# A graph network on one Trainium2 core: the root product and bias of the first relation layer become the initial value of its sums

## What is computed

```python
def rgcn_conv(x, edge_index, edge_type, W, W_root, b):
    src, dst = (edge_index[0], edge_index[1])
    seg = dst * N_REL + edge_type
    x_src = x[src]
    summed = jax.ops.segment_sum(x_src, seg, num_segments=N_NODES * N_REL)
    cnt = jax.ops.segment_sum(jnp.ones((src.shape[0],), x.dtype), seg, num_segments=N_NODES * N_REL)
    agg = summed / jnp.maximum(cnt, 1.0)[:, None]
    agg = agg.reshape(N_NODES, N_REL, x.shape[1])
    return jnp.einsum('nrd,rdh->nh', agg, W) + x @ W_root + b
...
x = jax.nn.relu(rgcn_conv(x, edge_index, edge_type, W1, root1, b1))
x = rgcn_conv(x, edge_index, edge_type, W2, root2, b2)
```

## Time and profile before

| | before |
|---|---|
| median of three runs | 8099.41 us |
| the profiled execution | 8102.81 us |
| its span, first to last instruction | 8100.9 us |
| GpSimd busy | 4914.7 us, 61% |
| TensorE busy (matmul) | 4193.5 us, 52% |
| VectorE busy | 2132.5 us, 26% |
| ScalarE busy | 1985.1 us, 25% |
| mean granted TensorE clock | 0.626 of full speed |

### The profile page before, as it was taken

One profiled execution on the slowest core, in us unless ns is written; L12 is line 12 of the kernel. 1 busy time (PEld: TensorE's weight loads), 2 busy tenths in 40 slices (PEclk: granted clock), 3 DMA queues, 4 the chain that ended last, 5 costly groups with the idle time before them and its releaser, 6 DMA issues.

```text
span 8100.9 us, 98203 instructions
## 1 busy us (share of the span) xinstructions
PE 4193.5 (52%) x18185; PEld 3399.4 (42%) x18186; DVE 2132.5 (26%) x7442; ACT 1985.1 (25%) x5480; POOL 4914.7 (61%) x5319
## 2 busy tenths in 40 slices
PE   5756667773333466666678333335433335333336
PEld 3355666533333345555544333333433334333334
DVE  6643333332222246666633000002000001000002
ACT  1100000010000034444422333331333332333331
POOL 0157777437777647777600777771677774777772
PEclk9956555786556566666657655556555655555556
DMA  4412222252222123333302222220122221222221
GB/s 162 162 39 57 58 57 58 98 211 52 52 52 52 43 61 85 84 84 84 76 0 112 66 52 52 52 52 14 53 52 52 52 52 34 55 52 52 52 52 30
DMA packets 282533, 529.06 MB, mean 65 GB/s; under 512 B 120299, under 2 KB 165695, under 8 KB 269519
## 3 DMA queue, kind: packets, MB, share of 16 engines
q0 software_dynamic: 159744, 330.88, 16.6%
q1 hardware_dynamic: 117918, 193.47, 6.8%
q10 hardware_dynamic: 4656, 2.79, 0.1%
HBM read 377.76 MB, written 149.02 MB: 65 GB/s over the span
## 4 chain that ended last, share of the span: by engine, by line
POOL 47%; issue 27%; PE 16%; DVE 5%; DMA 2%; DVEq 1%; ACT 1%; POOLq 1%; SPq 0%; ACTq 0%
POOL GB L585 45%; PE PS L872 3%; PE PS L1088 3%; PE PS L932 2%; PE PS L981 2%; PE PS L949 2%; PE PS L955 2%; POOL H L585 1%; DVE TOUT L1241 1%; DMA table<-TOUT 1%; DVEq L418 1%; PE PS L884 1%; DVE TOUT L1484 0%; DMA GB<-table_gat,IDX 0%; DVE H L1492 0%
## 5 line engine op out<-in xcount | busy, mean ns | idle before, releaser
L585 POOL DMA_INDIRECT GB<-table,IDX x4160 | 3946.2, 949 | 1426.4 <-issue 1354.8
L884 PE MATMUL PS<-OH,GB 128*128 128x128 f32 x8320 | 1953.2, 428 | 3054.8 <-DMA GB<-table,IDX 3033.5
L884 PEld LDWEIGHTS PS<-OH,GB 128*128 128x128 f32 x8320 | 1802.1, 328 | 3203.2 <-issue 2820.5
L1261 DVE TENSOR_TENSOR ACC<-ACC,PS 128x128 f32 x666 | 190.0, 285 | 4547.1 <-PE PS L884 4543.0
L684 ACT COPY IDX<-idx 128x8 int32 x520 | 102.3, 197 | 4103.4 <-PE PS L884 4103.1
L674 ACT ACTIVATE OH<-iota_f,local 128x128 f32<-128x128 f32 x2496 | 761.9, 387 | 0.0
L579 POOL COPY STG<-X 128x128 f32 x200 | 64.3, 322 | 1061.9 <-DVE X L1294 601.8
L585 POOL DMA_INDIRECT H<-table_gat,IDX x416 | 420.0, 1010 | 126.8 <-issue 124.3
L585 POOL DMA_INDIRECT GB<-table_gat,IDX x416 | 416.4, 1001 | 127.6 <-issue 120.7
L1088 PE MATMUL PS<-TOUT,OH 128*128 128x144 f32 x1664 | 425.9, 448 | 1.1 <-DVE TOUT L1484 1.1
L1088 PEld LDWEIGHTS PS<-TOUT,OH 128*128 128x128 f32 x1664 | 393.6, 329 | 2.7 <-issue 1.2
(11 more groups left out here) (248 smaller groups left out, 4111.0 us busy)
## 6 DMA issues: line engine op xcount, KB each, us to landing
table<-TOUT SPq DMA_DIRECT2D x100, 1024.0 KB, 3.9
GB<-table,IDX POOLq DMA_INDIRECT x4160, 2.5
TOUT<-local_row SPq DMA_DIRECT2D x104, 256.0 KB
table<-TOUT SPq DMA_DIRECT2D x50, 512.0 KB, 2.6
H<-etype_row SPq DMA_DIRECT2D x105, 64.0 KB
GB<-table_gat,IDX POOLq DMA_INDIRECT x416
H<-table_gat,IDX POOLq DMA_INDIRECT x416
table<-TOUT SPq DMA_DIRECT2D x20, 320.0 KB, 2.5
```

The source lines that it names most:

```text
L585: pool.indirect_dma_start(out=out[:, j, :], out_offset=None, in_=r.table.dram[:, :], in_offset=bass.IndirectOffsetOnAxis(ap=idx[:, j:j + 1 ...
L884: return nc.tensor.matmul(PS[:, bank, 0:P], GB[:, b, j * r.width:j * r.width + P], oh(b, j), **at)
```

## The change

The clearing of `sums` goes. After the degree products and before the first round, TensorE multiplies `X` by `root1` chunk by chunk into PSUM banks 1 to 7 in turn, and VectorE, behind the inversion of the counts, writes each chunk plus bias to `sums`. TensorE waits for all 16 of these before the round. Behind the round the node stage is replaced by 16 relus from `sums` to `H`, and the second table waits for those.

```diff
-        n_l0a = Stage("n_l0a", 2, 1, 0)
+        begun_pe, begun_dve, relu_dve = sem("begun_pe"), sem("begun_dve"), sem("relu_dve")
...
-        t_l0b = Table("t_l0b", H, WR[:, 0:2048], table16, [n_l0a.end(), (w2_in, 16)])
+        t_l0b = Table("t_l0b", H, WR[:, 0:2048], table16, [(relu_dve, CHUNKS), (w2_in, 16)])
...
+            for c in range(CHUNKS):
+                if c >= 7:
+                    pe.wait_ge(begun_dve, c - 6)
+                nc.tensor.matmul(PS[:, 1 + c % 7, 0:CHUNK], mat("L0_gnn_root1"), X[:, c * CHUNK:(c + 1) * CHUNK],
+                                 start=True, stop=True).then_inc(begun_pe, 1)
+            pe.wait_ge(begun_dve, CHUNKS)
+
             pe.wait_ge(rt_ready, 2)
...
-            node_products(n_l0a, [(0, mat("L0_gnn_root1"), X)], [], [edges_done(r_l0a)])
             multiply_table(t_l0b)
...
             dve.wait_ge(scratch, 64)
             dve.wait_ge(base_in, 80)
-            dve.memset(sums, 0.0)
             dve.memset(aux[0:R16, :], 0.0)
...
             dve.reciprocal(aux[0:R16, :], aux[0:R16, :]).then_inc(rt_ready, 1)
+
+            for c in range(CHUNKS):
+                dve.wait_ge(begun_pe, c + 1)
+                dve.tensor_scalar(sums[:, c * CHUNK:(c + 1) * CHUNK], PS[:, 1 + c % 7, 0:CHUNK], vec("L0_gnn_b1"), None, ALU.add)\
+                    .then_inc(begun_dve, 1)
+            dve.wait_ge(begun_dve, CHUNKS)
...
-            with dve.Fori(0, PAIRS) as i:
-                st = n_l0a
-                for h in range(2):
-                    dve.wait_ge(st.pe, st.pe_at(i, 1, h))
-                    dve.scalar_tensor_tensor(T0[h], bank(0, h), vec("L0_gnn_b1"), sums[:, chunk(i, h)], ALU.add, ALU.add).then_inc(st.dve, 1)
-                for h in range(2):
-                    dve.wait_ge(st.dve, st.dve_at(i, 1, h))
-                    dve.tensor_scalar(H[:, chunk(i, h)], T0[h], 0.0, None, ALU.max).then_inc(st.dve, 1)
+            dve.wait_ge(r_l0a.agg_free, TWO + TILES)
+            for c in range(CHUNKS):
+                here = slice(c * CHUNK, (c + 1) * CHUNK)
+                dve.tensor_scalar(H[:, here], sums[:, here], 0.0, None, ALU.max).then_inc(relu_dve, 1)
```

More of the change, by code:

```diff
@@ L823, in _ @@
                 pe.sem_inc(t.made, 2)
-            for st in (n_l0a, n_l0b, n_l1, n_l2a, n_l2b, n_l3a, n_l3b):
+            for st in (n_l0b, n_l1, n_l2a, n_l2b, n_l3a, n_l3b):
                 pe.sem_inc(st.pe, 1)
```

## The result

The changed kernel took 8290.57 us (median of 5 runs, 8282.36 to 8298.45) against 8099.41 of the kernel before in the same comparison: a ratio of 1.024, 95% interval 1.0229 to 1.0252. It is slower by 191 us where 17 fewer were forecast, and far outside the range of 8066 to 8097. The profiled execution took 8294.1 us, its span is 8292.2 us.

The account below looks back on a forecast made before the run. GpSimd's gathers were taken to set the edge rounds' pace, with the change acting only in seams between stages. -6.9 + 9.7 - 22.8 + 2.2 = -17.8 us gave 8082 us against 8099.4, range 8066 to 8097.

Parts of the forecast that it names:

- seams: Places between stages where one's end releases the next; the edited ones, with the clock, were to sum to -17.8 us.
- Start: Start of the first table: without clearing `sums`, VectorE is earlier; 6.9 us saved, bounds 5.4 and 8.2.
- Initial value: Ahead of the first edge round: 16 evictions behind the inversion delay the look-ups; 9.7 us added, bounds 5.8 and 15.0.
- Behind the round: Between last addition and first staging copy: 28.02 us of node stage give way to 5.2 us, 22.8 saved.
- Clock: Second table: without the removed stage's warming, TensorE starts at the low clock; 2.2 us lost.
- rival C: VectorE's instruction stream: moved attention loop's returns take longer, up to 8159 us; chance 0.12, of it 0.07 over 0.2% slower.
- the short loops of the other rounds show no such stall: In rival C: only the attention loop's returns, 3.2 us each, showed VectorE standing still with nothing waited for.
- 33 instructions ahead of the round: In rival C: VectorE's program grows by some 33 instructions there, a few behind it, so every later loop moves.
- 24 x 3.2: Rival C's price in the attention loop: returns twice as long add 77 us.
- 8159 us: Rival C's time if each attention loop return needs twice as long, 77 us on top.
- chance of 0.07: Chance given to a time over 0.2% longer, through rival C's longer attention loop return.
- if a stage without any edit gets longer: Sign against the prediction: it is wrong if any unedited stage gets longer or shorter; no size given.

Follow-up runs that it names:

- the one without the stream's effect: Changed kernel plus 1 idle semaphore increment ahead of the first table and 111 ahead of the degree sums; 8087.06 us against 8113.6 before, 0.997.
- before_m2: Kernel before with two VectorE semaphore increments moved behind the first table's loop, which then starts at 319; 8281.26 us, 1.0223.
- before_g20: Kernel before with 20 idle increments ahead of VectorE's wait for the degree sums, attention loop on a border; 8098.31 us, 1.000.
- before_s432: Kernel before with 111 idle increments ahead of the first table and 17 ahead of the degree sums, first loop at 432; 8095.9 us, 0.9996.
- one and four fillers: Changed kernel with one or four semaphore increments nobody waits for ahead of the first table; 8106.97 us (1.0011) and 8076.01 us (0.9968) against the kernel before.
- 16 fillers: Kernel before with 16 idle increments ahead of the degree sums, attention loop 4 instructions ahead of a border; 8130.2 us, 1.0036.
- 433: Kernel before with 112 idle increments ahead of the first table and 16 ahead of the degree sums, first loop at 433; 8212.09 us, 1.0139.
- 440: Kernel before with 119 idle increments ahead of the first table and 9 ahead of the degree sums, first loop at 440; 9835.71 us, 1.015.
- 447: Kernel before with 126 idle increments ahead of the first table and 2 ahead of the degree sums, first loop at 447; 9887.42 us, 1.0189.

## Why the prediction was wrong

**The sum of the seams was right**, -20.0 us against -17.8, though in the initial value two errors met by luck. Part by part, forecast and then the trace of the kernel after:

- Start: -6.9, bounds 5.4 and 8.2; measured -7.8 at block 2 (and -7.0 at the inversion of the kernel whose loop isn't disturbed). Block 1 started at 75.57 and took 3.67 us, the gain from the shorter pause included.
- Initial value: +9.7; measured +9.5. The evictions ended 10.0 us behind the inversion (forecast 10.7). The two errors: each eviction took 0.60 us, from 9.61 / 16 of both rows, and not 0.55, and TensorE, on the 9 chunks left, was hardly behind (it kept VectorE waiting 0.49 us). Batch 0 gave back 0.6 us (look-ups 3.77 to 3.51, sums 3.75 to 3.46) and not 1.0: it was warm only in part.
- Behind the round: -22.8; measured -23.1 (28.02 to 4.89 from the last addition's end). Relus 4.53 us (forecast 4.5), the wait for the own addition 0.03 (0.35), the wake-up 0.33 (0.34).
- Clock: +2.2; measured +1.4 in the kernel after and +2.9 in the one without the stream's effect. The second table starts with weight loads of 0.34 us and reaches 0.19 at 1737.28, 3.2 us after its start. By the Trainium skill (TensorE: Matmul & The Clock Gate, What's actually happening) the slow state is the default, and this trace agrees. But the forecast took from one trace that the removed stage leaves TensorE at the high clock. In three of the seven traces of kernels that keep it (`before_m2`, `before_g20`, `before_s432`) the second table too has first weight loads of 0.34 us, and takes 173.0 us from first to last matmul instead of 171.3 (172.8 in the kernel after, 174.2 in the one without the stream's effect). So a part of this term is there without the change.

**The step that failed is rival C.** It had the right mechanism (the instruction stream), and failed in three of its terms. First its place: it looked at the attention loop alone, since only that one stalled in the trace of before, and let the others go with "the short loops of the other rounds show no such stall". That none stalled showed that each was held from one return to the next, not that it would stay so when moved: the first table's loop stood at 321, and at 319 it stalls. Second its direction: it counted what the change adds (33 instructions ahead of the round), and not the two that it takes away ahead of the first table, which decided 183 us. (The attention loop itself moved by 16.) Third its price: "24 x 3.2" for a longer return was near for the attention loop (a second stall of 3.0 us at 23 returns, 68.5 us), but most of that is hidden, for the round grew by 18.7 us only; and for the first table's loop, which lies on the path, a return cost 8.0 us, 183 us in all: a pause of 8.0 that covers a wait of 2.2, and 2 more through TensorE's lower clock. The 8159 us that it named were thought of as its far end.

The chance of 0.07 for a time longer by over 0.2% was therefore too low by its own reasoning: that the place of loops in the stream weighs was seen, and "nothing in the trace says how the place weighs" should have widened the range, as for any cost that no row bounds.

What the forecast said would prove it wrong, "if a stage without any edit gets longer", is what happened, twice.

**What stays open.** The +4.8 us between the second table and the attention table in the kernel after have no cause that was shown. From last matmul to first matmul that stretch took 1156.8 us there, 1156.2 and 1157.3 with one and four fillers, but 1150.3 in the changed kernel without the stream's effect, and 1147.7 to 1153.8 in the kernels without the change. So the change itself doesn't need it, and what does is open. Other loops give no sign of a stall. In the traces of the kernels before and after, of the one with 16 fillers and of the changed ones with 1 and with 1 and 111 fillers, no engine's loop but the two of VectorE takes as much as 0.5 us from its branch back to the next record. A stall inside such a loop was not looked for.

## What to carry over

Before an edit that adds or removes instructions ahead of a loop, count where the loop begins and ends in its engine's program, in instructions; a loop whose blocks are just held can fall out of that by one instruction, on either side, and cost more than the edit is worth. When a stage without an edit gets longer, look at the packets of the instruction queue and for idle time with nothing waited for at the loop's top, and test with increments that nobody waits for, in an idle place: 111 ahead of the first table cost nothing here. And judge an edit only with the loops put back in their place: this one saves 24 us (15 to 34) with the loops put back, and costs 191 without.

## What the runs showed of the hardware

- VectorE's instructions come in packets of 8192 bytes, 128 instructions, and borders at 320, 448, 704 and 1600 fit all runs of these programs, all 64 more than a multiple of 128. A loop of 272 instructions over three such blocks returned without a stall (321, 320, 323, 432); over four it loaded five packets at each of its 23 returns (319, 433, 440, 447). The Trainium skill (Runtime: NRT & Kernel Launch, Instruction fetch mechanics) speaks of blocks of 16 KiB (256 instructions), of which two are held. By borders every 256 instructions either 319 and 320 would differ or 432 and 433, not both; the measurement decides for 128. The section also says that a taken branch to a block not held stalls, and the pauses of 5.6 us behind the branch agree.
- The pause at such a return: 5.84 us with 15 instructions ahead of the next border, 6.79 with 8, 8.02 with 1, of which 0, 1.0 and 2.3 us are a second stall at that border, whose far side started 8.0 to 8.3 us after the branch each time. What it cost this loop is another number, since it covers a wait and slows TensorE: 4.9, 6.3 and 8.2 us a return, from the first table's 426.4, 459.2 and 503.0 us less 314.4, over 23.
- A loop of 556 instructions stalled at each of its 23 returns in every run, from the branch to the next record for 2.7 to 3.0 us (medians of the traces), and five blocks or six made no difference (8098.31 against 8096.32 us). With 4 instructions ahead of a border it had a second stall of 3.0 us. Why its first stall is shorter than the 5.6 us of the first table's loop is not shown.
- A semaphore increment that nobody waits for cost nothing that could be measured where its engine idles (128 of them: 0.9996, 0.9986 to 1.0006).
- The kernel before took 8096 to 8114 us in the first comparisons and 9698 in the last, so a time means something only beside its own comparison. The record names chip 11 for the last and also for one in which it took 8096.32, so a slower chip is not shown as the cause. The time lies in the edge rounds: the last round's gathers took 1223.8 us in the kernel with 440 and 1050.0 in the one with 433, while the branch back of the first table's loop took 5.65 and 5.63 us.
